# Moving norm and routing work across stage borders in a two-layer mixture-of-experts block on one core

## What is computed

```python
x = x + tanh(g_xattn[0]) * L0_xattn(layernorm(x), ctx)     # 16 heads of 16, 375 keys
x = x + tanh(g_ffn[0])   * L0_ffn(layernorm(x))            # 14 routed experts (top 2) + 2 shared
x = x + tanh(g_xattn[1]) * L1_xattn(layernorm(x), ctx)     # one head of 256
x = x + tanh(g_ffn[1])   * L1_ffn(layernorm(x))            # 4 experts (top 2), final layer norm * on_g + on_b
```

## Time and profile before

| | us |
|---|---|
| median of three runs | 877.27 |
| the profiled execution, time of the program | 875.93 |
| its span, first to last instruction | 873.9 |
| last DVE work of stage 1 ends / first work of stage 2 | 294.57 / 296.03 |
| stage 3 ends / first work of stage 4 | 701.71 / 702.79 |
| PE busy, share of the span | 83% |
| DVE, ACT, POOL busy | 65%, 52%, 47% |
| mean granted clock of TensorE | 0.925 |

### The profile page before, as it was taken

One profiled execution on the slowest core, in us unless ns is written; L12 is line 12 of the kernel. 1 busy time (PEld: TensorE's weight loads), 2 busy tenths in 40 slices (PEclk: granted clock), 3 DMA queues, 4 the chain that ended last, 5 costly groups with the idle time before them and its releaser, 6 DMA issues. The chain is left out here.

```text
span 873.9 us, 20368 instructions
## 1 busy us (share of the span) xinstructions
PE 728.4 (83%) x6673; PEld 557.3 (64%) x6703; DVE 565.8 (65%) x1381; ACT 458.6 (52%) x949; POOL 412.5 (47%) x554
## 2 busy tenths in 40 slices
PE   3777999999988499897999999578989659999940
PEld 2454666666666499896777777456767536777730
DVE  6665777777785759984544555278667446556756
ACT  3644666666655466682333433144544346777742
POOL 5896788888700327884000000575533714313254
PEclk9998999999999669998999999789889879999985
DMA  7335444443300327774222221588532213323333
GB/s 177 95 90 125 117 113 117 114 113 79 90 15 2 102 94 247 250 240 130 74 80 85 80 81 60 145 222 220 157 96 78 69 59 119 110 70 93 106 113 100
DMA packets 87661, 98.92 MB, mean 113 GB/s; under 512 B 17260, under 2 KB 77132, under 8 KB 87564
## 3 DMA queue, kind: packets, MB, share of 16 engines
q1 hardware_dynamic: 63468, 66.10, 25.8%
q0 software_dynamic: 16432, 24.66, 10.5%
q10 hardware_dynamic: 7664, 6.89, 2.7%
HBM read 61.03 MB, written 24.38 MB: 98 GB/s over the span
## 5 line engine op out<-in xcount | busy, mean ns | idle before, releaser
L782 DVE TENSOR_REDUCE a_mx<-ps 112x2 f32<-112x750 f32 x128 | 120.1, 939 | 52.1 <-PE ps L400 50.2
L672 POOL DMA_DIRECT2D a_stkK<-a_KS x248 | 118.7, 487 | 21.5 <-issue 15.4
L642 ACT ACTIVATE a_Pf<-ps 125x672 f32<-125x672 f32 x128 | 89.9, 728 | 14.5 <-PE ps L344 13.1
L51 PE MATMUL ps<-f_w2hi,f_hh 128*128 (+1 forms) x292 | 81.8, 280 | 3.7 <-DVE f_hl L1552 3.7
L51 PE MATMUL ps<-f_w2hi,f_hl 128*128 (+1 forms) x292 | 81.5, 279 | 0.0
L51 PE MATMUL ps<-f_w2lo,f_hh 128*128 (+1 forms) x292 | 81.4, 279 | 0.0
L2386 ACT ACTIVATE f_rf<-ps,f_ln 128x128 f32<-128x128 f32 x136 | 54.5, 453 | 31.0 <-PE ps L2336 31.0
L1547 DVE CAST f_hh<-ps 128x512 bf16<-128x512 f32 x41 | 28.3, 691 | 64.5 <-PE ps L1283 64.5
L1840 POOL MEMSET a_half<- 112x2 f32 x1 | 0.1, 93 | 146.1 <-POOLq L88 146.1
L1207 POOL DMA_INDIRECT f_xd<-xn,pos x32 | 57.3, 1790 | 22.7 <-issue 22.7
L2346 PE MATMUL ps<-f_w,f_rf 128*128 x272 | 64.5, 380 | 0.1
(11 more groups left out here) (378 smaller groups left out, 2089.0 us busy)
## 6 DMA issues: line engine op xcount, KB each, us to landing
f_xg<-f_xd SPq DMA_DIRECT2D x75, 128.0 KB, 2.2
f_yd<-f_yo SPq DMA_DIRECT2D x75, 128.0 KB, 1.7
a_raw<-F_w SPq DMA_DIRECT2D x18, 512.0 KB, 5.5
f_raw<-F_w SPq DMA_DIRECT2D x14, 512.0 KB, 4.6
a_ctxF<-ctxT SPq DMA_DIRECT2D x16, 375.0 KB, 3.2
a_cR<-ctx SPq DMA_DIRECT2D x16, 375.0 KB
a_stkK<-a_KS POOLq DMA_DIRECT2D x248, 23.4 KB, 2.0
f_xd<-a_zero ACTq DMA_DIRECT2D x13, 384.0 KB, 3.2
```

What stands on the lines that cost most here:

```text
L51: ins = nc.tensor.matmul(out, l, r, start=first and i == 0, stop=last and i == len(steps) - 1)
L642: nc.scalar.activation(Pf[:, j % PB], psST[:C, j % 2, :, 0:SC * T], ACT.Exp, scale=DH ** -0.5).then_inc(exp_done, 1)
L672: pool.dma_start(stkK[SIDE * h + DH * a:SIDE * h + DH * (a + 1), w.slot, jj], KS[2 * DH * jj + DH * h:2 * DH * jj + DH * (h + 1), w.odd, p ...
L782: nc.vector.reduce_max(mx[:, n.odd, j // JJ, :, j % JJ], maxima_of(n, j)[:T, :, :S], AX).then_inc(mx_red, 1)
```

## The change

Three parts. At the first border (stage 1 to 2) twelve of the sixteen rows are normed in stage 1. DVE takes the moments of rows 0 to 10 in the last `emit`, aggregates rows 0 to 11 and forms `sc`'s argument (`squares`); POOL takes the power; then ACT writes seven rows of `xn`, POOL three and DVE two. The last four rows get their scale at the end of stage 1 (POOL again) and are written by DVE at the start of stage 2. Stage 2 takes `rstd` by a power on POOL, PE turns groups 0 to 2 through six banks without a wait, and the first weight splits of ACT and DVE stand behind the splits of `xT`. Second, the factor on `f1.on` moves from DVE at i = 8 to ACT behind the whole of stage 3. Third, the last four of the first half's 16 scatters move from i = 17 of stage 3 to the start of stage 4, and the second half's gates, ranks, places and blocks' experts all stand ahead of the block loop.

```diff
@@ l0_attention @@
+        EARLY = GB * LAST
+        XN_POOL, XN_DVE = (1, 5, 9), (3, 7)
+        XN_ACT = [b for b in range(EARLY) if b not in XN_POOL + XN_DVE]
@@ scalar @@
+                act.wait_ge(a_full, KD * LAST)
+                act.wait_ge(nm_done, 1)
+                for r in XN_ACT:
+                    nc.scalar.activation(k.xn[:, r, :], k.xs[:, r, :], ACT.Identity, bias=k.nm[:, r:r + 1],
+                                         scale=k.sc[:, r:r + 1]).then_inc(early_act, 1)
+                act.wait_ge(early_act, len(XN_ACT))
@@ gpsimd @@
+                def scales(lot, rows):
+                    pool.wait_ge(sc_ready, lot + 1)
+                    nc.gpsimd.tensor_tensor(k.sc[:, rows], k.sc[:, rows], half[:, 0:1].broadcast_to([T, rows.stop - rows.start]),
+                                            ALU.pow).then_inc(sc_done, 1)
...
+                scales(0, first_rows)
+                pool.wait_ge(sc_done, 1)
+                pool.wait_ge(a_full, KD * LAST)
+                for r in XN_POOL:
+                    nc.gpsimd.tensor_scalar(k.xn[:, r, :], k.xs[:, r, :], k.mv[:, r, 0:1], k.sc[:, r:r + 1],
+                                            ALU.subtract, ALU.mult).then_inc(early_pool, 1)
+                scales(1, last_rows)
@@ vector @@
-                        if b is None and p is not None and s == 3:
-                            for r in range(3):
+                        if b is None and p is not None and s in (1, 3, 5):
+                            for r in range(0, 4) if s == 1 else range(4, 7) if s == 3 else range(7, EARLY - 1):
                                 row_moments(r)
...
+                row_moments(EARLY - 1)
+                for r in range(EARLY):
+                    aggregate(r)
+                squares(first_rows)
+                add_rows(EARLY)
+                dve.wait_ge(sc_done, 1)
+                dve.wait_ge(a_full, KD * LAST)
+                nc.vector.scalar_tensor_tensor(k.nm[:, first_rows], k.mv[:, first_rows, 0], -1.0, k.sc[:, first_rows],
+                                               ALU.mult, ALU.mult).then_inc(nm_done, 1)
+                for r in range(EARLY + 1, B):
+                    row_moments(r - 1)
+                    if r - EARLY <= len(XN_DVE):
+                        early_row(XN_DVE[r - EARLY - 1])
                     add_rows(r)
-                    row_moments(r - 1)
+                    aggregate(r - 1)
                 row_moments(B - 1)
-                for r in range(B):
-                    dve.wait_ge(y_st, r + 1)
-                    nc.vector.bn_aggr(k.mv[:, r, :], stats[:, r, :]).then_inc(y_var, 1)
+                aggregate(B - 1)
+                squares(last_rows)
@@ l0_experts, gpsimd @@
-                pool.wait_ge(norm_done, 1)
-                for b in range(2, B, GB):
-                    nc.gpsimd.tensor_scalar(k.xn[:, b, :], k.xs[:, b, :], k.mv[:, b, 0:1], sc[:, b:b + 1],
-                                            ALU.subtract, ALU.mult).then_inc(xn_pool, 1)
+                pool.wait_ge(var_ready, 1)
+                nc.gpsimd.tensor_tensor(k.rstd[:], var[:], half[:, 0:1].broadcast_to([T, B]), ALU.pow).then_inc(rstd_done, 1)
                 for l in LOADS[:LOW_POOL]:
                     split2(l)
@@ tensor @@
-                    pe.wait_ge(xn_dve, (g + 1) * GB // 2)
-                    pe.wait_ge(xn_act, g + 1)
-                    pe.wait_ge(xn_pool, g + 1)
-                    if g >= 2:
-                        pe.wait_ge(x_lo, g - 1)
-                    bank = 2 * (g % 2)
+                    if g == LAST:
+                        pe.wait_ge(xn_dve, GB)
+                        pe.wait_ge(x_lo, 1)
+                    bank = bank_of(g)
@@ scalar @@
-                split1(LOADS[0])
-                high2(LOADS[0])
                 for g in range(NG):
                     act.wait_ge(x_full, g + 1)
...
-                for l in LOADS[1:FIRST_LOADS]:
+                act.wait_ge(rw_in, 32)
+                for l in LOADS[:FIRST_LOADS]:
                     split1(l)
                     high2(l)
@@ vector @@
+                for b in range(GB * LAST, B):
+                    ts(k.xn[:, b, :], k.xs[:, b, :], k.mv[:, b, 0:1], k.sc[:, b:b + 1], ALU.subtract, ALU.mult).then_inc(xn_dve, 1)
+                ts(var[:], k.mv[:, :, 1], LN_EPS, None, ALU.add).then_inc(var_ready, 1)
...
-                split1(LOADS[0])
                 for g in range(NG):
                     dve.wait_ge(x_hi, g + 1)
...
+                link(nc.vector.reciprocal(red2[:], k.sc[:]))
+                dve.wait_ge(rstd_done, 1)
+                link(tt(rms[:], k.rstd[:], red2[:], ALU.mult))
+                dve.wait_ge(rw_in, 32)
+                split1(LOADS[0])
                 split1(LOADS[1])
@@ l1_attention @@
+LEFT = 4
-        SCATTERS = {13: 4, 14: 5, 16: 1, 17: 6}
+        SCATTERS = {13: 4, 14: 5, 16: 1, 17: 6 - LEFT}
@@ scalar, behind the loop @@
+                act.wait_ge(vec_in, 64)
+                nc.scalar.activation(f1.on[:], f1.on[:], ACT.Copy, scale=k.tg_f[:T, 1:2]).then_inc(on_done, 1)
@@ vector @@
-                    if i == 8:
-                        dve.wait_ge(vec_in, 64)
-                        ts(f1.on[:], f1.on[:], k.tg_f[:T, 1:2], None, ALU.mult).then_inc(on_done, 1)
@@ l1_experts, tensor @@
+                pe.wait_ge(mb_done, 1)
+                rank_products(nc, f1, rank).then_inc(rank_done, 1)
                 expert[0] = expert_of(0)
@@ gpsimd @@
+                for i, b in [(i, b) for b in range(HB) for i in range(2)][2 * HB - LEFT:]:
+                    scatter(i, b)
@@ vector, ahead of the block loop @@
+                dve.wait_ge(exp_done, 1)
+                gates(nc, f1, link).then_inc(gates_done, 1)
+                dve.wait_ge(gates_done, 1)
+                dve.wait_ge(rank_done, 1)
+                nc.vector.tensor_copy(f1.rank[:], rank).then_inc(rank_read, 1)
+                dve.wait_ge(rank_read, 1)
+                bases(nc, f1, link, 1)
+                places(nc, f1, link, 1).then_inc(pos_done, 1)
+                block_experts(nc, f1, link, 1).then_inc(bexp_done, 1)
                 for n in STEPS:
```

More of the change, by code:

```diff
@@ L128, in l0_attention @@
         eps, warm = sb("eps", [T, 1], F32), sb("warm", [T, 1], F32)
+        half = sb("half", [T, 1], F32)
         SIDE, KEYS, DOT = P // 2, 3 * DH, 3 * DH + 2
@@ L185, in l0_attention @@
             sem(s) for s in ("afull", "ahi", "alo", "yfull", "yused", "yst", "yvar", "actq"))
+        half_set, sc_ready, sc_done, nm_done, early_act, early_pool, early_dve = (
+            sem(s) for s in ("halfset", "scready", "scdone", "nmdone", "earlyact", "earlypool", "earlydve"))
         k_sp, k_pool = ([sem(f"kin{q}{i}") for i in range(4)] for q in ("sp", "pool"))
@@ L720, in _ @@
                 pool.wait_ge(offset_done, B)
+                pool.wait_ge(half_set, 1)
+                scales(0, first_rows)
[5 more added lines that the diff above has]
+                scales(1, last_rows)
+                pool.wait_ge(early_pool, len(XN_POOL))
+                pool.wait_ge(sc_done, 2)
             @block.vector
@@ new lines, in squares, with early_row @@
+                def squares(rows):
+                    dve.wait_ge(y_var, rows.stop)
+                    nc.vector.tensor_scalar(k.sc[:, rows], k.mv[:, rows, 1], 1.0 + RMS_EPS, RMS_EPS * LN_EPS,
+                                            ALU.mult, ALU.add).then_inc(sc_ready, 1)
+                def early_row(r):
+                    nc.vector.tensor_scalar(k.xn[:, r, :], k.xs[:, r, :], k.mv[:, r, 0:1], k.sc[:, r:r + 1],
+                                            ALU.subtract, ALU.mult).then_inc(early_dve, 1)
@@ L1069, in l0_experts @@
         z = sb("z", [P, HID], F32)
-        eps = sb("eps", [T, 2], F32)
-        root, sc, nmean, rms = (sb(n_, [T, B], F32) for n_ in ("root", "sc", "nmean", "rms"))
+        half = sb("half", [T, 1], F32)
+        var, rms = (sb(n_, [T, B], F32) for n_ in ("var", "rms"))
         rt = sb("rt", [P, KD, E], F32)
@@ L1113, in l0_experts @@
         FIRST_LOADS = 3
+        LAST = NG - 1
+        bank_of = lambda g: 2 * (g % LAST)
         LOW_POOL = 3
@@ L1348, in _ @@
             def _(act):
-                act.wait_ge(eps_set, 2)
-                nc.scalar.activation(root[:], k.mv[:, :, 1], ACT.Sqrt, bias=eps[:, 0:1]).then_inc(root_done, 1)
-                act.wait_ge(ms_done, 1)
-                nc.scalar.activation(rms[:], red[:], ACT.Sqrt, bias=eps[:, 1:2]).then_inc(rms_done, 1)
-                act.wait_ge(norm_done, 1)
-                for b in range(0, B, GB):
-                    nc.scalar.activation(k.xn[:, b, :], k.xs[:, b, :], ACT.Identity, bias=nmean[:, b:b + 1],
-                                         scale=sc[:, b:b + 1]).then_inc(xn_act, 1)
-                act.wait_ge(rw_in, 32)
                 def split1(l):
@@ L2276, in l1_experts @@
         STEPS = range(-2, BLOCKS + 6)
-        GATES, RANK, PLACE, SCATTER = 0, 1, 2, 3
+        SCATTER = 3
```

67 lines of the change are left out of this document (20 added, 47 removed).

## The result

| | median, us | runs, us | ratio to before (95% interval) |
|---|---|---|---|
| before, beside the change | 878.44 | 875.96 to 880.93 (4) | |
| changed kernel | 866.68 | 861.73 to 870.57 (4) | 0.9873 (0.9835 to 0.9912) |
| changed kernel again, in a later set (e12) | 867.31 | 864.94 to 870.40 (6) | 0.9891 (0.9852 to 0.9930) |

The changed kernel is about 1.2% faster, some 10 to 11 us. The prediction was 867.0 (862.5 to 871.5).

What follows compares the result with a forecast made beforehand. No engine alone sets the time; waits at the first border, in stage 3 and at the last border do. Gains of 2.7 + 5.5 + 2.1 = 10.3 us take the median from 877.27 to 867.0, range 862.5 to 871.5.

Steps and rivals of the forecast that it cites:

- Part 1 (a): First border, end of stage 1: stage 2 starts at 297.6 us, 1.6 later than before.
- (b): Start of stage 2 to end of logits: 15.8 us against 22.0, with 0.3 of stall; logits end 4.6 earlier.
- rival 1: Stage 2: unbroken transposes raise the clock, the 96 products run faster, 4 us more, 863; chance 0.1.
- (c): Choice in stage 2: loses 1.9 us beside POOL's third split, ends at 321.1 against 323.8.
- Part 2: Stage 3, factor on `on`: 5.5 us earlier, 2.8 from the instruction and 2.7 from the clock.
- the second half: Stage 3: PE's clock no longer falls behind the moved factor, giving 2.7 us more.
- Rival 3: Stage 3 gives only the instruction, the clock falls elsewhere: 7.6 us in all, 869.7; chance 0.15.
- Part 3: Last border: first load 1.1 us later, blocks 0 to 3 give 3.2 back, 2.1 earlier in sum.

Runs made afterwards that it cites:

- e12: The changed kernel once more, word for word, in a later set; ratio 0.9891, median 867.31 us.
- e6: Changed kernel with the cast of small constants moved from the end of i = 4 to the end of i = 5; ratio 0.9834, median 860.31 us.
- e3: Kernel before with only the first-border change (early norm, powers for square roots, unbroken transposes); ratio 0.9965, 3.1 us faster.
- e1: Kernel before with only the factor on the last norm's weights moved from DVE to ACT behind stage 3; ratio 0.9931, 6.0 us faster.
- e5: Kernel before with the factor kept on DVE but moved from the end of i = 8 to i = 14; ratio 0.9960, 3.5 us faster.
- e9: Changed kernel with constants at i = 5, third low part on DVE, second expert's low part behind choice, exponential before third weights' high part; ratio 0.9785.
- e7: Changed kernel with DVE's low part of the second expert's first weights moved behind the first choice; ratio 0.9901.
- e8: Changed kernel with the third low part of the second weights moved from GpSimd to DVE, behind the ranks; ratio 0.9885.
- e10: Changed kernel with transposes of the third and fourth group waiting for DVE's low parts again, in two pairs of banks; ratio 0.9904.
- e11: Changed kernel with constants at i = 5 and the third low part on DVE behind the ranks; ratio 0.9800, median 860.46 us.
- e4: Kernel before with the whole second choice ahead of the block loop, but no scatter left behind the last border; ratio 1.0011.
- e2: Kernel before with only the last-border change: four scatters behind the border, whole choice ahead of the block loop; ratio 1.0003.

## Why the prediction was right, and where it was right by luck

Old order and new order below are groups of traces that share the code of the stretch; each number is the difference of two starts or ends in a timeline.

| stretch | old | new | moved | predicted |
|---|---|---|---|---|
| end of the low parts to first load of expert rows (stage 2) | 111.1, 111.1, 111.4, 111.6, 113.3 (mean 111.7) | 105.7, 107.4 (the change), 108.6 (e6), 108.7 (e3) (mean 107.6) | 4.1 earlier | 2.7 |
| minimum of i = 7 to that of i = 11 | 30.8 (four traces) | 25.4 (e1, e5, e6, e9, e12), 25.9 to 26.0 (first trace of the change, e7, e8, e10, e11) | 4.9 to 5.4 earlier | 5.5 |
| minimum of i = 11 to the last product's end | 37.7 to 38.2 (before, e1 to e4) | 38.1 to 38.2 (e6, e7, e8), 39.6 and 39.7 (the change), 40.3 to 41.9 (e9, e10, e11) | 0 to 4 later | 0 |
| last product's end to block 3's turn | mean 30.9 (30.3 to 31.7) | 28.2 to 28.6 (e2, e6 to e12, the change: nine traces) | 2.4 earlier | 2.1 |

With 1.6 later in the third row the sum is 4.1 + 5.4 - 1.6 + 2.4 = 10.3, the number predicted. That it agrees to the tenth is luck: the first row gave 1.4 more than I said and the third took 1.6, for which I had no term. The change's own two traces, read the same way, give 11.4 and 10.7; the two measured ratios give 11.2 and 9.6. The first trace shows 14.2 (875.93 - 861.73). Of that, 2.2 is the earlier end of the low parts in stage 1, and about 2.5 its short row of scatters.

**Part 1 (a), the border: right.** 1.3 later against 1.6. Both powers came as worked out (2.30 and 1.03). `nm` wasn't held by a GpSimd row (0.17), and GpSimd's rows took 1.21 each and not 1.44, so they were done (292.26) before DVE's argument for the last four (292.54), and the last power waited 0.37 for DVE. That power ended last, at 293.65, as I had said, and stage 2 started 1.4 behind it.

**(b), start of the stage to the end of the logits: right in e3, wrong in all others of the new order.** In e3 it took 15.9 us (15.8 predicted), with 0.57 of stall ahead of the last group. Even there the stall had another cause: DVE waited 1.94 us for the router's weights to land, not for the power. In the changed kernel it took 12.4 and 10.2 (e12), since the clock rose. That is rival 1, which I gave 0.1. Its premise came true; its time (863) didn't. Granted clock of e12 in three stretches of 1 us (busy time of each engine, then the clock ahead of the last two columns); PE has nothing but transposes up to 301.2 us:

```profile
298.00:299.00 1.00, 1.00 (x8) 1.00 (x7) 0.11 (x1) 0.85 (x1) 1.00 (x1) 0.50 0.33 27
299.00:300.00 1.00, 1.00 (x9) 1.00 (x8) 0.96 (x3) 0.58 (x1) 1.00 (x1) 0.59 0.86 205
300.00:301.00 1.00, 0.99 (x11) 0.81 (x10) 0.92 (x2) 0.88 (x2) 0.72 (x1) 1.00 0.84 311
```

0.50 is the level of 1.2 GHz and 1.00 that of 2.4. It rose inside the stage's first 7.7 us in eight of nine traces of the new order (all but e3) and in none of five of the old. My argument against was the earlier trace rows: before, PE worked from 305.80 to 318.0 without a break and the clock stayed low. The row was right (so it is in all five traces of the old order), but it didn't carry over to the new order. The Trainium skill ("TensorE: Matmul & The Clock Gate", part 4), which I called in support, says that transposes don't count as PE being busy in the same way; these rows speak against that. What makes the clock rise stays open: e10 has a break in the transposes and rises; PE's idle time before them is 5.0 to 7.5 us in the new order and 8.8 in all five traces of the old, but e3, with 5.0, is the one that doesn't rise. No experiment varied that alone.

Rival 1 said that this would give 4 us and end at 863. It did not, and that is the step the prediction lacked altogether. DVE has the low part of the second expert's weights ahead of the choice. I left it out of the sum because its 1.42 lay well ahead of the logits' end before. Now it runs beside GpSimd's two splits and takes 4.6, so DVE is free only 14.3 to 15.2 us into the stage wherever that low part stands ahead of the choice and the transposes have no break, though the logits end at 10.2 to 12.4 (16.4 in e10 with logits at 13.5; 16.1 in e3, where both end together). Of the 3.5 to 5.7 that the clock gave, 0.8 to 1.7 arrived. Two omissions nearly cancelled; e9 shows it from the other side, with the choice at 10.3 once that low part is out of the way.

**(c), the choice: right.** 7.5 to 7.7 in five traces of the new order (7.7 predicted, 5.8 before). e8 shows the cause by taking it away: 5.79 without GpSimd's split. e8 didn't turn it into time, since its scatters took 2.2 longer. That is the price of its cure, a DVE pass close to the scatters, and not a sign that an earlier choice is worth nothing: e9, with the same long row of scatters (68.4), starts them 1.5 earlier than e8 and has its first load 1.6 earlier.

**Part 2: right, in both halves.** 5.4 against 5.5. e5 separates cause from cure: the same instruction on the same engine costs 0.58 away from the split, and the clock doesn't fall. The weight of the second half shows in e6 again: 2.8 of instruction and 2.6 to 4.0 behind it. Rival 3 is out in all ten traces without the factor at i = 8: the clock from i = 9 to 11 is 1.00 in each. In five of them these two rounds take 13.2 and not 12.7, at full clock; the cause is open.

**Part 3: right on the sum, both terms too small.** The first load came 1.7 later (8.8 behind the last product against 7.1), where I said 1.1: stage 4 starts 1.6 behind DVE's copy (684.83 to 686.41), and GpSimd needs another 0.68 before its first scatter there (687.09). I had it start with the stage. What the loop gave back is 3.9 (14.6, the mean of four, to 10.68), where I took 3.2 from one trace.

**Open.** In both traces of the changed kernel, in e9, e10 and e11, but not in e6, e7 and e8, which run the same code there, 1.5 to 3.8 us are lost behind i = 15. This is the term that the prediction had at nothing. PE and ACT of e11 at that place:

```profile
674.01 1.59 PE L1958 MATMUL ps<-a_pT,a_cR 125*128 125x112 f32 x12
677.86 0.36 ACT L2084 ACTIVATE a_mT<-ps 128x224 f32<-128x224 f32 x1 [2.93 <-DMA a_stkK<-a_KS]
678.27 1.48 PE L2002 MATMUL ps<-a_V,a_mT 128*112 128x256 f32 x4 [2.67 <-issue]
```

ACT's copy starts 2.3 us after the last product that is recorded (675.60), at full clock; in e6 it starts with it (672.34 and 672.37). The releaser named has nothing to do with this stage. Some product before it must have been held up, and the trace doesn't say by what. The kernel before and e1 to e5, which have at most one part of the change, don't show it either, so the whole change may favour it. No experiment tested that.

## What to carry to other kernels

When an instruction is moved to make room, look at every instruction that shares its new stretch with GpSimd's long subtractions, not only at those that are moved: here one DVE pass grew from 1.4 to 4.6 us and swallowed most of a gain that another engine had made. Before handing a stalled instruction to another engine, try it at another place on its own (e5), and look for its siblings: e6 found as much again with one number. And a gain ahead of a queue that other work paces (the scatters here) must be read behind the queue, not ahead of it: the work that was moved to win it may slow the queue, as in e8.

## What the runs showed of the hardware

- GpSimd's two-input subtraction of 128x1024 (2.13 us) holds up some DVE operations and not others. A cast of 112x24 (2.61 us, 0.14 elsewhere), a comparison of 112x224 with a constant (2.08, 0.28 elsewhere) and operations with two inputs in SBUF (2.13 to 2.26 for 112x224, 0.39 elsewhere) wait it out. Operations whose first input lies in PSUM take as long beside it as alone: the low part of `xT` 1.08, an update of `xs` 0.48; so does a reduction (0.39). Timelines of the kernel before, POOL and then DVE, with two low parts of `xT` in 2.09:

```profile
305.22 2.13 POOL L1193 TENSOR_TENSOR f_w2lo<-a_raw,f_w2hi 128x1024 bf16<-128x1024 f32 x1
304.56 2.09 DVE L1467 TENSOR_TENSOR xT_lo<-ps,xT_hi 128x896 bf16<-128x896 f32 x2 [0.32 <-ACT xT_hi L1378]
```

- GpSimd's power holds DVE up only at its start, if at all. Beside the power of 112x16 (298.62 to 301.52 in e3) DVE's cast of 128x28 took 0.18 and its two-input subtraction of 128x28 took 0.19, both some 2 us into it. In the earlier trace rows the two-input product that started 0.3 into the power of eight took 0.62 (as in all 14 traces), and the next one, inside the same power, took 0.15:

```profile
658.91 0.62 DVE L2174 SCALAR_TENSOR_TENSOR a_nm<-mv,rstd 112x2 f32<-112x2 f32 x1
659.45 0.15 DVE L2178 SCALAR_TENSOR_TENSOR a_nm<-a_mv,a_rstd 112x2 f32<-112x2 f32 x1
```

  Beside GpSimd's rows of `xn` DVE's own took 0.40 and 0.47. The Trainium skill ("SBUF — State Buffer", "SBUF: two separate sides") has the shared port pair held for the full instruction, whichever engine has it. The rows beside the subtraction agree, those beside the power don't.
- GpSimd's power takes 0.69, 1.03, 1.67, 2.30 and 2.90 us for 2, 4, 8, 12 and 16 columns: 0.37 and 0.16 a column.
- The clock can rise, fall and rise again while PE never stops: in the changed kernel PE is busy throughout from 295.1 to 314.0. The granted clock is 1.00 from 301.3 to 304, behind the transposes; it falls while PE runs the logits' products (14 columns each), is 0.50 from 305 to 311, and is 1.00 again from 312, while PE runs products of 224 columns. Three level changes in one such stretch make any price read off one trace uncertain by several us.
